# GpSimd makes every eighth drive product of a Mamba scan; B, C and dt in one projection; two parts of B placed by DMA

## The reference, cut to what matters

```python
xc = silu(causal_conv(xs) + conv_b)              # xs, z: halves of LayerNorm(seq) @ in_w
dbl = xc @ xproj_w
dt, Bm, Cm = dbl[..., :6], dbl[..., 6:22], dbl[..., 22:]
delta = softplus(dt @ dt_w + dt_b)
A = -exp(A_log)
dA = exp(delta[..., None] * A)
dBx = delta[..., None] * Bm[:, :, None, :] * xc[..., None]
h[t] = dA[t] * h[t-1] + dBx[t]                   # for 192 channels x 16 states
y = (einsum('blds,bls->bld', h, Cm) + Dp * xc) * silu(z)
seq = seq + y @ out_w
```

## Time and profile before

| what | value |
|---|---|
| median of 3 runs | 4724.49 us (4716.68 to 4725.94) |
| the profiled execution | 4725.55 us |
| its span | 4723.4 us |
| the phase with the scans | about 83 to 3133 us of the span |
| busy over the span | TensorE 4159.9 us, VectorE 3580.9, GpSimd 2469.5, ScalarE 2405.8 |
| granted TensorE clock, mean | 0.953 |

### The profile page before, as it was taken

One profiled execution on the slowest core, in us unless ns is written; L12 is line 12 of the kernel. 1 busy time (PEld: TensorE's weight loads), 2 busy tenths in 40 slices (PEclk: granted clock), 3 DMA queues, 4 the chain that ended last, 5 costly groups with the idle time before them and its releaser, 6 DMA issues. The chain is left out here.

```text
span 4723.4 us, 44868 instructions
## 1 busy us (share of the span) xinstructions
PE 4159.9 (88%) x13922; PEld 1790.8 (38%) x13922; DVE 3580.9 (76%) x4409; ACT 2405.8 (51%) x3937; POOL 2469.5 (52%) x1988
## 2 busy tenths in 40 slices
PE   6999999999999999999999999841989889888964
PEld 2333333333333333333333333311546546555543
DVE  3999999999999999999999999974115415414345
ACT  4666666666666666666766676621013222312223
POOL 3778887888778877887788778740000000000000
PEclk8999999999999999999999999985999999999976
DMA  3444444444444444444444444433010020000000
GB/s 91 141 130 137 136 143 134 135 137 145 135 133 138 142 137 137 136 138 141 136 138 133 144 132 138 126 88 88 21 38 21 6 53 17 17 15 4 17 0 14
DMA packets 135882, 462.03 MB, mean 98 GB/s; under 512 B 20783, under 2 KB 23282, under 8 KB 133822
## 3 DMA queue, kind: packets, MB, share of 16 engines
q1 hardware_dynamic: 135646, 459.18, 32.6%
HBM read 433.64 MB, written 20.97 MB: 96 GB/s over the span
## 5 line engine op out<-in xcount | busy, mean ns | idle before, releaser
L664 POOL TENSOR_TENSOR prod<-states,c_rows 128x512 f32<-128x512 f32 x1536 | 1939.6, 1279 | 589.2 <-DVE states L596 573.6
L596 DVE TENSOR_TENSOR_SCAN states<-decay,carry,bpsum 128x512 f32<-128x512 f32 x1536 | 1937.8, 1262 | 0.0
L353 PE MATMUL ypsum<-prod,identity 128*128 128x512 f32 x3072 | 1582.4, 596 | 0.4 <-POOL prod L664 0.3
L455 ACT ACTIVATE decay<-delta,decay_rate 128x512 f32<-128x512 f32 x1536 | 1078.4, 716 | 722.1 <-DVE states L596 623.4
L583 DVE TENSOR_TENSOR bpsum<-bpsum,dx 128x512 f32<-128x512 f32 x1536 | 1034.9, 674 | 89.8 <-PE bpsum L346 71.7
L346 PE MATMUL bpsum<-b_rows,select 96*128 96x512 bf16 x1536 | 594.2, 387 | 167.6 <-DVE states L596 166.0
L353 PEld LDWEIGHTS ypsum<-prod,identity 128*128 128x128 f32 x3072 | 590.2, 194 | 309.4 <-issue 175.3
L346 PEld LDWEIGHTS bpsum<-b_rows,select 96*128 96x128 bf16 x1536 | 147.7, 96 | 1072.8 <-DVE states L596 669.4
L1063 PE MATMUL convp<-img_hi,w_hi 96*96 96x512 f16 (+1 forms) x1568 | 485.3, 387 | 59.0 <-PEq L1441 43.1
L1411 DVE SCALAR_TENSOR_TENSOR x<-convp,unscale,x_group 96x1024 f32<-96x1024 f32 x16 | 20.4, 1278 | 407.9 <-PE convp L1063 407.9
L1063 PE MATMUL convp<-img_hi,w_lo 128*96 128x512 f16 (+1 forms) x896 | 276.0, 387 | 0.0
(11 more groups left out here) (215 smaller groups left out, 4531.6 us busy)
## 6 DMA issues: line engine op xcount, KB each, us to landing
c_rows<-c_map SPq DMA_DIRECT2D x512, 512.0 KB, 3.7
c_rows<-c_map SPq DMA_DIRECT2D x512, 256.0 KB, 3.9
x_in<-in_x SPq DMA_DIRECT2D x16, 384.0 KB, 6.0
fused_map<-fused SPq DMA_DIRECT2D x16, 384.0 KB, 5.1
work<-fused_map SPq DMA_DIRECT2D x4, 1536.0 KB, 9.6
x<-in_x SPq DMA_DIRECT2D x4, 1536.0 KB, 15.8
x_biased_map<-work SPq DMA_DIRECT2D x4, 1536.0 KB, 7.1
x_group<-x_biased_map SPq DMA_DIRECT2D x16, 384.0 KB, 3.7
```

Of the source, the lines that this page charges most:

```text
L353: pe.matmul(ypsum[:, group % Y_BANKS, :], identity[:, :], prod[:, n % P_RING, :], start=s == 0, stop=s == STATES - 1).then_inc(summed, 1)
L455: act.activation(decay[:, n % RING, :], delta[k % 2][:, g, :], ACT.Exp, scale=decay_rate[:, ORDER[k][0], g, s:s + 1]).then_inc(decay_ready, 1)
L596: dve.tensor_tensor_scan(states[:, n % H_RING, :], decay[:, n % RING, :], bpsum[:, n % B_BANKS, :], carry[:, at, u:u + 1], ALU.mult, ALU.a ...
L664: pool.tensor_tensor(prod[:, n % P_RING, :], states[:, n % H_RING, :], c_rows[:, n // C_STATES % C_RING, n % C_STATES, :], ALU.mult).then_ ...
```

## The change

Units with n mod 8 = 7 (six a step, 192 in all: slots 7, 15, 23, 31, 39, 47) are taken another way. SyncE broadcasts their row of B from DRAM into `b_wide`; GpSimd makes the drive (`drive_unit`, L766) in slot n-2, ahead of its product in that slot; ScalarE writes their decay into the free bank of bpsum, in slot n-3; VectorE does no product for them, and its scan reads the decay from PSUM and the drive from SBUF. TensorE makes no broadcast for them.

The projection becomes one chain of three matmuls onto 76 rows (B, C, dt) in bank 0. The rows of B and C go to DRAM together. B stands there once, so its middle and low parts are made on the first 32 partitions and DMAs bring them to rows 32 to 95 of `b_rows` (`move_b`). The pieces from `proj` on stand two to four slots earlier in the tables. `tmp2` is one buffer instead of three.

```diff
+EVERY, POOL_LEAD, B_RING, B_AHEAD = 8, 2, 2, 19
 EARLY = {
...
-    "proj": [30, 31, 32, 33, 34, 35], "hi": [35, 36], "rest": [37], "mid": [38], "low": [39],
-    "dt": [37, 40, 41], "v": [38, 41, 42], "soft": [39, 40, 41, 42, 43, 44],
+    "proj": [30, 31, 32], "hi": [33], "rest": [34], "mid": [35], "low": [36],
+    "dt": [34, 37, 36], "v": [35, 38, 37], "soft": [36, 37, 38, 39, 40, 41],
 LATE = {
...
-    "proj": [29, 29, 30, 30, 31, 31], "hi": [32, 32], "rest": [33], "mid": [34], "low": [35],
-    "dt": [34, 36, 37], "v": [35, 37, 38], "soft": [37, 38, 39, 40, 41, 42],
+    "proj": [29, 30, 31], "hi": [32], "rest": [33], "mid": [34], "low": [35],
+    "dt": [33, 36, 35], "v": [34, 37, 36], "soft": [35, 36, 37, 38, 39, 40],
-SP_AT = 8
+SP_AT, SP_ROWS_AT, SP_MOVE_AT = 8, 16, 17
+def on_pool(n):
+    return n % EVERY == EVERY - 1
...
# SyncE
+                def load_b(n):
+                    k, u = divmod(n, STEP_UNITS)
+                    g, s = divmod(u, STATES)
+                    i = n // EVERY
+                    if u == EVERY - 1:
+                        sp.wait_ge(rows_stored, 16 * (k + 1))
+                    if i >= B_RING:
+                        sp.wait_ge(driven, i - B_RING + 1)
+                    broadcast_rows(0, k, g, s, 1, b_wide[:, i % B_RING, :], b_loaded[i % B_RING])
+                def move_b(step):
+                    sp.wait_ge(mid_ready, step + 1)
+                    sp.dma_start(b_rows[step % 2][BC_ROWS:2 * BC_ROWS, :], b_mid[:, :]).then_inc(b_moved, 16)
+                    sp.wait_ge(bank0_read, USE[0, step - 1, PROJ] + 1)
+                    sp.dma_start(b_rows[step % 2][2 * BC_ROWS:, :], b_low[:, :]).then_inc(b_moved, 16)
...
# TensorE
-                        last = pe.matmul(mm[0:rows, bank, :], w_proj[:, layer, g, off:off + rows],
+                        last = pe.matmul(mm[0:DT_ROW + 2 * RANK, 0, :], w_proj[:, layer, g, :],
                                          xc[step % 2][:, g, :], start=g == 0, stop=g == GROUPS - 1)
...
-                    if 0 <= t + B_LEAD < UNITS:
+                    if 0 <= t + B_LEAD < UNITS and not on_pool(t + B_LEAD):
                         broadcast_b(t + B_LEAD)
...
# ScalarE
-                        act.wait_ge(bank_full[i], USE[i, w, PROJ] + 1)
-                        if i == 0:
-                            rows = slice(DT_AT, DT_AT + 2 * RANK)
-                            act.activation(dt_rows[rows, :], mm[rows, 0, :], ACT.Copy).then_inc(dt_copied, 1)
-                            act.activation(b_rows[step % 2][:, :], mm[0:DT_AT, 0, :], ACT.Copy).then_inc(hi_ready, 1)
...
+                        act.wait_ge(bank0_full, USE[0, w, PROJ] + 1)
+                        rows = slice(DT_ROW, DT_ROW + 2 * RANK)
+                        act.activation(dt_rows[rows, :], mm[rows, 0, :], ACT.Copy).then_inc(dt_copied, 1)
+                        if step > 0:
+                            act.wait_ge(rows_stored, 16 * step)
+                        act.activation(bc32[:, :], mm[0:2 * BC_ROWS, 0, :], ACT.Copy).then_inc(rows_ready, 1)
+                        act.activation(b_rows[step % 2][0:BC_ROWS, :], mm[0:BC_ROWS, 0, :], ACT.Copy).then_inc(hi_ready, 1)
...
# VectorE
+                    if on_pool(n):
+                        dve.wait_ge(driven, i + 1)
+                        dve.wait_ge(wide_ready, i + 1)
+                        by, add = bank, drive[:, i % B_RING, :]
...
                     for i in due(plan["rest"], at):
-                        dve.wait_ge(dt_copied, step + 1)
                         dve.wait_ge(hi_ready, step + 1)
...
-                    if 0 <= t + 1 < UNITS:
+                    if 0 <= t + 1 < UNITS and not on_pool(t + 1):
                         scale_unit(t + 1)
...
# GpSimd
+                def drive_unit(n):
+                    k, u = divmod(n, STEP_UNITS)
+                    g, i = u // STATES, n // EVERY
+                    if i >= B_RING:
+                        pool.wait_ge(scanned, n - EVERY * B_RING + 1)
+                    pool.wait_ge(dx_ready, 3 * k + g + 1)
+                    pool.wait_ge(b_loaded[i % B_RING], 16 * b_landings(i))
+                    pool.tensor_tensor(drive[:, i % B_RING, :], b_wide[:, i % B_RING, :], dx[k % 2][:, g, :],
+                                       ALU.mult).then_inc(driven, 1)
...
+                    if 0 <= t + POOL_LEAD < UNITS and on_pool(t + POOL_LEAD):
+                        drive_unit(t + POOL_LEAD)
                     if 0 <= t < UNITS:
                         unit(t)
```

More of the change, by code:

```diff
@@ L102, in bank_uses @@
             for stage in stages:
-                if stage != STEP2 or bank == 1:
+                if bank == (1 if stage == STEP2 else 0 if stage == PROJ else bank):
                     table[bank, w, stage] = count[bank]
@@ L109, with others, unit_of, b_landings @@
 USE = bank_uses()
+def on_pool(n):
+    return n % EVERY == EVERY - 1
+def others(n):
+    return (EVERY - 1) * (n // EVERY) + n % EVERY
+def unit_of(other):
+    return EVERY * (other // (EVERY - 1)) + other % (EVERY - 1)
+def b_landings(load):
+    return sum(2 if EVERY * i % STEP_UNITS >= 2 * STATES else 1 for i in range(load % B_RING, load + 1, B_RING))
 def c_landings(load):
@@ L170, in mamba_phase @@
         b_rows = [sb(f"b_rows{p}", [DT_AT, CHUNK], BF16) for p in range(2)]
-        c32 = sb("c32", [BC_ROWS, CHUNK])
-        dt_rows = sb("dt_rows", [DT_AT + 2 * RANK, CHUNK])
+        b_mid = sb("b_mid", [BC_ROWS, CHUNK], BF16)
+        b_low = sb("b_low", [BC_ROWS, CHUNK], BF16)
+        bc32 = sb("bc32", [2 * BC_ROWS, CHUNK])
+        b_wide = sb("b_wide", [128, B_RING, CHUNK])
+        drive = sb("drive", [128, B_RING, CHUNK])
+        dt_rows = sb("dt_rows", [DT_ROW + 2 * RANK, CHUNK])
         yy = sb("yy", [128, GROUPS, CHUNK])
@@ L283, in load_x, with broadcast_rows @@
                                  dram["x"][:, 2 * pair:2 * pair + 2, c * CHUNK:c * CHUNK + CHUNK]).then_inc(x_loaded[pair], 16)
+                def broadcast_rows(kind, k, g, first, count, tile, loaded):
+                    for r0, r1, b in (((0, 128, 0),), ((0, 128, 1),), ((0, HALF, 0), (HALF, 128, 1)))[g]:
+                        rows = bc_dram[k % 2, kind, b, first:first + count, :].rearrange("s n -> (s n)")
+                        sp.dma_start(tile[r0:r1], rows.unsqueeze(0).to_broadcast([r1 - r0, count * CHUNK])).then_inc(loaded, 16)
                 def load_c(i):
@@ L315, in _ @@
                 load_x(1, 0)
-                store_c(0)
+                store_rows(0)
+                move_b(0)
                 for i in range(C_RING):
                     load_c(i)
+                for i in range(B_RING):
+                    load_b(EVERY * i + EVERY - 1)
                 for w in range(STEPS):
@@ L561, in _ @@
                     w, at, coming, done, current = now(t)
-                    if 0 <= t + DECAY_LEAD < UNITS:
+                    if 0 <= t + B_LEAD < UNITS and on_pool(t + B_LEAD):
+                        unit(t + B_LEAD)
+                    if 0 <= t + DECAY_LEAD < UNITS and not on_pool(t + DECAY_LEAD):
                         unit(t + DECAY_LEAD)
```

115 lines of the change are left out of this document (65 added, 50 removed).

## The result

The changed kernel took 4796.39 us in the median of 4 runs (4792.45 to 4799.14), against 4723.89 (4716.68 to 4725.94) for the kernel before: 1.0156 times as long, 95% interval 1.0138 to 1.0173. Forecast were 4756 us and at most 4792. The direction is right. The loss is more than twice what was forecast, 72 us where it was 32.

A forecast was written before the change was run, and what follows sets the result against it. VectorE was taken as the bound, TensorE for part of each step. Terms summed to +1.4 us a step, +40 over 29 steps, -8 elsewhere: +32, giving 4756 us; forecast band 4738 to 4772, wider range 4690 to 4792.

The forecast's parts named there:

- (A): Slots 16 to 26, where TensorE is the bound: one broadcast fewer, -0.2 us a step.
- (C): Slot 38 to slot 2, where VectorE is the bound: two products fewer, -1.16 us a step.
- (D): Slot 2 to TensorE's slot 16: scan 15 waits for GpSimd's drive; layer 1 +1.75, layer 0 +0.45, average +1.1 us.
- (B): Slot 26 to the end of slot 37: VectorE waits for ScalarE's copies before the first subtraction, +1.65 us a step.
- S(2)+28.6: Forecast start of TensorE's slot 16: 28.6 us after VectorE can go on from the scan of slot 2.
- The start: Before the steps: three matmuls saved, some 2.6 us, and two more setup loads paid, about 1 us.
- the two LATE steps: Steps with a LATE step ahead: no normalisations before drive 15 and three matmuls fewer, about -2 us each.
- Drive 15 in time: Rival: GpSimd's drive for slot 15 is not late, the wait before the first subtraction stays; 4712 us, chance 0.09.
- Neither wait: Rival: VectorE waits neither before the first subtraction nor for drive 15; -2.7 us a step, 4637 us, chance 0.07.
- `rest` does not wait, drive 15 does: Rival: no wait before the first subtraction, but scan 15 waits for GpSimd; 4681 us, chance 0.06.
- Rival 5: GpSimd not level with VectorE in slot 2, its queue one us later: +1 us a step, 4786 us, chance 0.13.
- The third wait named: VectorE's waits for TensorE's broadcasts of B over the phase: to fall from 71.7 to under 40 us.

The follow-up runs named there:

- the run without drives: The changed kernel with all 48 products on VectorE and no GpSimd drives, projection, tables and moves of B kept: 4776.15 us.
- the run with three slots: The changed kernel with GpSimd's drives made three slots ahead of their scan instead of two: 4714.29 us.
- the fillers: The changed kernel with nine extra zero-adding matmuls on TensorE in slot 16 of layer 1 steps: 4777.37 us.
- five slots of lead: The changed kernel with GpSimd's drives made five slots ahead of their scan instead of two: 4708.0 us.
- both edits: The changed kernel with drives five slots ahead and the first subtraction two slots later (one in the LATE table): 4633.36 us.

## Why the prediction was right and wrong, by its steps

**(A) and (C)**, one broadcast and two products fewer, and **(D)**: the changed kernel less the run without drives shows them together, 97.11-96.55=+0.56 in layer 1 and 96.52-97.25=-0.73 in layer 0. Forecast were -0.2-1.16+1.75=+0.39 and -0.91. D's wait was forecast at 3.7 and 4.3 and is 3.55 and 3.58 (with 0.59 more at drive 7 in layer 0, which makes 4.17). Right, with the layer 1 step dearer as foreseen because TensorE could have gone on earlier there. That VectorE's wait alone is not the price is shown by the run with three slots.

**(B)**: forecast +1.65 from a wait of about 2.6; measured +1.68 from 2.52 to 2.66. ScalarE's timeline shows the three copies that the prediction timed:

```profile
1043.05 0.59 ACT L605 ACTIVATE dt_rows<-mm 12x512 f32<-12x512 f32 x1
1043.66 0.59 ACT L608 ACTIVATE bc<-mm 64x512 f32<-64x512 f32 x1
1044.16 0.57 ACT L609 ACTIVATE b_rows<-mm 32x512 bf16<-32x512 f32 x1
```

From the first to the subtraction at 1044.76 are 1.71 us, against 1.81 in the sum.

**The step that failed** is D's sentence "Slot 16 begins at S(2)+28.6: layer 1 +1.75", which costs the wait by when TensorE starts again and takes for granted that it then works at its old speed. That it would stand there was in the prediction's own numbers: S(2)+28.6 against 26.88 before, less the 0.45 of two broadcasts, is 2.2 us; 2.38 were measured. What the runs showed in its place is a slot 16 at half the speed. In 11 of 14 layer 1 steps it ran at half clock, some 1.68 us dearer and twice 3.1. That is 21 of the 43 us between the two sums, shown by the fillers. The mean clock in the table of before (0.953) told that it falls somewhere; the millisecond of the earlier trace rows has 1.00, and I asked of no new wait what it does to the clock.

**The start, running step 0 and the two LATE steps** hold 15 us more; for the start and the LATE steps even the sign was wrong. In running step 0 GpSimd is later still, since it comes straight out of the first softplus. VectorE waits 1.14 and 4.81 there (forecast was an ordinary step):

```profile
100.40 1.28 DVE L670 TENSOR_TENSOR_SCAN states<-bpsum,carry,drive 128x512 f32<-128x512 f32 x1 [1.14 <-POOL drive L766]
...
118.87 1.28 DVE L670 TENSOR_TENSOR_SCAN states<-bpsum,carry,drive 128x512 f32<-128x512 f32 x1 [4.81 <-issue]
```

With five slots of lead this step is 92.29, less than the 92.73 of before, so the drives' lateness is its cause; part of it is the clock, which fell in slot 16 here as well. For the two LATE steps I had -2 each because "no normalisations before drive 15". But VectorE waits 1.2 for drive 15 there, 0.4 to 0.6 for each of drives 7, 23, 39 and 47, and for `hi` 3.60 where the earlier trace rows have 1.15:

```profile
259.21 0.69 DVE L709 TENSOR_TENSOR mm<-mm,b_rows 32x512 f32<-32x512 f32 x1 [3.60 <-ACT b_rows L609]
```

Of the +2.9 up to the first scan most is not shown to be the change's: the run with fillers, the same program there but for one memset, has its first scan at 82.86. Before it is 83.31, and in the changed kernel's profiled execution 86.19. The remaining +0.25 a step in the 28 in the middle (6.9 us) is what the four terms are off together.

**The rivals.** Drive 15 in time was put at 4712 and is 4708.0 (five slots). Neither wait was put at 4637 and is 4633.4 (both edits). "`rest` does not wait, drive 15 does" was put at 4681, and is 4765.6. It has the clock wrong like the forecast, and a mechanism of its own besides. Term (C) had GpSimd "level with VectorE again in slot 1", and I carried that over to a case without the wait of slot 34. There the softplus is late for GpSimd by 2.60 us, drive 47 is late as well, and of the 2.55 a step that the missing wait was to give (from +1.65 to -0.9) only 0.67 came (96.52 to 95.85 in layer 0). Rival 5 (4786) is the nearest number of all and not what happened: product 2 started at 1075.19, 0.24 after the end of scan 2, with GpSimd level. The third wait named, for broadcasts, was to fall under 40 and is 63.1; nothing in the sum hung on it.

## What to carry to other kernels

A task given to an engine with slack on average must be placed by that engine's queue at that slot, and not a fixed number of slots ahead of its use: the same drives cost time two slots ahead and gave 66 us when five ahead and with the other wait gone. A wait is priced by the engine that is the bound in that stretch (three slots ahead VectorE waited 1.2 to 1.8 us for next to nothing), and if that engine is TensorE, by what it does after the wait as well. When one of two waits is taken away, ask who was catching up in it (here ScalarE, on which GpSimd hung).

## What the runs showed of the hardware

- TensorE ran at half clock right after it had stood 2.38 us in 11 of 14 equal steps, and at full clock in the other three; after 0.53 us it fell in none of the 14 layer 0 steps, and with 2.10 of the idle time filled by matmuls with zeros, in none of 14. Between slots 37 and 47, where the longest wait was 1.5 us, it fell in 18 of 28 steps of both layers. The Trainium skill (TensorE: Matmul & The Clock Gate, HAM oscillation — how this bites in real kernels) tells of a kernel that pays this after waits for DMAs in every tile; the trace agrees that waits between dense stretches can be enough, here one of 2.4 us for another engine. What one costs depends on who is the bound: 1.68 us or more in slot 16, nothing between slots 37 and 47.
- GpSimd's two-input operations of 128x512 float32 follow each other at 1.23 us also over 22 in a row. The Trainium skill (GPSIMD Engine Reference, 3.1 Elementwise) gives a figure from which 1.11 is an estimate; by it the wait for drive 15 would have been an estimated 1.1 and 1.7 us, and it was 3.6.
- A scan with its decay in PSUM and its drive in SBUF takes 1273 ns, one with them the other way round 1263.
